# Layer norms 1 to 3: the low part of the turned tokens by a TensorE product with a negative unit matrix and a ScalarE copy, in place of a VectorE subtraction

## What is computed

```python
x = L0_attn_data                                   # 1024 x 512, fp32
x = x + _L0_attn_ref(_layernorm(x), ...)           # product with a block-masked weight, 512 x 512
x = x + _L0_ffn_ref(_layernorm(x), ...)            # product with an int4 weight, and a bias
x = x + _L1_attn_ref(_layernorm(x), ...)           # NF4 weights with low-rank terms: (q+k+v)/3, out, gate/up, down
x = x + _L1_ffn_ref(_layernorm(x), ...)            # FP4-rounded activations and weights, gated MLP
```

## Time and profile before

| what | us |
|---|---|
| time, median of 3 runs | 836.36 (834.82 to 837.74) |
| the profiled execution, its own time | 842.19 |
| its span (first to last instruction) | 840.8 |
| PE busy | 722.5 (86%) |
| DVE busy | 582.3 (69%) |
| ACT busy | 430.1 (51%) |
| POOL busy | 191.4 (23%) |
| mean granted TensorE clock | 0.945 of full speed |

### The profile page before, as it was taken

The page is one execution under the profiler, slowest core; times in us unless marked ns, Lnnn a source line. Parts: engine busy times, 40 slices in busy tenths (PEclk is TensorE's granted clock), DMA queues, the critical chain, the costliest instruction groups (busy, mean ns, idle before and its releaser), DMA issues.

```text
span 840.8 us, 11246 instructions
## 1 busy us (share of the span) xinstructions
PE 722.5 (86%) x4112; PEld 537.4 (64%) x4112; DVE 582.3 (69%) x1107; ACT 430.1 (51%) x549; POOL 191.4 (23%) x176
## 2 busy tenths in 40 slices
PE   1796755878999998989998999778999799959998
PEld 1564421656777766667665777566777588957886
DVE  4899978644598788889897984568363333567873
ACT  3765747457777767877656511264322221225452
POOL 0213000003253452635544543222001200000000
PEclk9999966799999999999998999989899899988999
DMA  8644668767366686758755110211001210200001
GB/s 279 214 140 154 204 209 268 264 218 244 111 193 208 198 246 208 237 175 265 222 166 161 62 47 27 62 39 53 23 1 38 60 47 26 76 10 12 26 26 38
DMA packets 56040, 110.55 MB, mean 131 GB/s; under 512 B 9889, under 2 KB 20801, under 8 KB 55985
## 3 DMA queue, kind: packets, MB, share of 16 engines
q1 hardware_dynamic: 42560, 78.43, 28.9%
q10 hardware_dynamic: 9040, 17.30, 6.1%
q0 software_dynamic: 4384, 14.09, 5.9%
HBM read 91.65 MB, written 18.15 MB: 131 GB/s over the span
## 4 chain that ended last, share of the span: by engine, by line
PE 51%; DVE 27%; issue 8%; DMA 6%; ACT 6%; SPq 1%; ACTq 0%; DVEq 0%
PE bank L1106 13%; PE bank L1107 13%; PE bank L1108 13%; DVE hot L1747 3%; PE bank L1213 2%; DMA wide_buf<-in_down_flat 2%; DVE bank L1773 2%; ACT hot L1501 2%; DVE x L1870 2%; PE bank L1394 2%; PE bank L1226 1%; DVE q_a L1820 1%; DMA codes<-c 1%; DVE q_r L1814 1%; DVE gm L1789 1%
## 5 line engine op out<-in xcount | busy, mean ns | idle before, releaser
L1501 ACT ACTIVATE hot<-rep,levels 128x2048 f16<-128x2048 f16 x96 | 193.6, 2056 | 19.7 <-ACT c L1464 10.1
L1106 PE MATMUL bank<-zt_h,w_h 128*128 128x512 f32 (+1 forms) x232 | 93.2, 402 | 2.5 <-DVE zt_l L1858 2.0
L1108 PE MATMUL bank<-zt_h,w_l 128*128 128x512 f32 (+1 forms) x232 | 91.2, 393 | 0.0
L1107 PE MATMUL bank<-zt_l,w_h 128*128 128x512 f32 (+1 forms) x232 | 91.0, 392 | 0.0
L1213 PE MATMUL bank<-hot,diag 128*32 128x512 f16 x1160 | 79.2, 399 | 8.2 <-DVE hot L1747 5.6
L1106 PE MATMUL bank<-w_h,xq_h 128*128 128x512 f32 (+1 forms) x192 | 75.4, 393 | 5.8 <-DVE w_l L1888 3.5
L1107 PE MATMUL bank<-w_l,xq_h 128*128 128x512 f32 (+1 forms) x192 | 73.5, 383 | 0.0
L1108 PE MATMUL bank<-w_h,xq_l 128*128 128x512 f32 (+1 forms) x192 | 73.1, 381 | 0.0
L2013 POOL TENSOR_TENSOR q_a<-q_a,q_m 128x384 f32<-128x384 f32 (+3 forms) x34 | 35.7, 1050 | 109.2 <-DVE q_m L1641 109.2
L1213 PEld LDWEIGHTS bank<-hot,diag 128*32 128x32 f16 x1160 | 26.1, 98 | 52.2 <-issue 26.0
L1106 PE MATMUL bank<-w_h,at_h 128*128 128x512 f32 x112 | 48.3, 431 | 7.8 <-DVE x L1870 5.0
(11 more groups left out here) (219 smaller groups left out, 1674.8 us busy)
## 6 DMA issues: line engine op xcount, KB each, us to landing
rep<-codes SPq DMA_DIRECT2D x58, 512.0 KB, 4.6
codes<-c SPq DMA_DIRECT2D x29, 256.0 KB
raw<-in_codes_gu_t ACTq DMA_DIRECT2D x14, 512.0 KB, 4.6
sc<-in_scales_gu_t SPq DMA_DIRECT2D x56, 128.0 KB, 4.4
raw<-in_codes_attn_t ACTq DMA_DIRECT2D x8, 512.0 KB, 4.7
raw<-in_codes_down_t ACTq DMA_DIRECT2D x7, 512.0 KB, 5.7
sc<-in_scales_down_t SPq DMA_DIRECT2D x28, 128.0 KB, 3.0
wide_buf<-in_gate_flat SPq DMA_DIRECT2D x5, 512.0 KB, 4.7
```

Source lines behind the costliest of these rows:

```text
L1106: PE.matmul(psum, lh, rh, start=first, stop=False, **kw)
L1107: PE.matmul(psum, lh, rl, start=False, stop=False, **kw)
L1108: return PE.matmul(psum, ll, rh, start=False, stop=last, **kw)
L1501: S.activation(hots[plan.slot[hot_ring(t), (t, m)]][:], codes_in_place(t), ACT.Relu, bias=bias, scale=slope).then_inc(sem("ramp_act"), 1)
```

## The change

For layer norms 1 to 3 (`ln < PE_LOWS`, which is 3) the DVE subtraction is gone. A new step `tlow` has two halves. On PE one matmul with the matrix `minus` (minus one on the diagonal) and `zt_h` of this tile adds `-zt_h` to the bank that holds the turned tile; the four transposes of the tile are now an open group of accumulation for this. On ACT a copy then takes the bank, which now holds the low part, into `zt_l`. The bank comes free after that ACT copy, and `product` and `o_mm` wait for it. In the list of steps `tsplit` of tile n-1 now stands ahead of `norm` of tile n+1, and `tlow` behind it. Layer norm 4 keeps the DVE subtraction, under the name `tdiff`. `minus` is built at the start of the program, and no longer at the start of the last phase.

```diff
+PE_LOWS = 3
+def split_done(ln, n):
+    return ("act", "tlow", ln, n) if ln < PE_LOWS else ("dve", "tdiff", ln, n)
...
             p.add("turn", ln, n)
-            turn_bank(("ln", ln, n), ("dve", "tsplit", ln, n))
+            turn_bank(("ln", ln, n), split_done(ln, n))
+            if ln < PE_LOWS and turned is not None:
+                p.add("tsplit", ln, turned)
             if n + 1 < NT:
                 norm(ln, n + 1)
+            if ln >= PE_LOWS and turned is not None:
+                p.add("tsplit", ln, turned)
             if turned is not None:
-                p.add("tsplit", ln, turned)
+                p.add("tlow" if ln < PE_LOWS else "tdiff", ln, turned)
                 yield turned
             turned = n
...
                 for k in range(KD):
                     cols = slice(256 * (k // 2) + k % 2, 256 * (k // 2) + 256, 2) if ln == 1 else tok(k)
-                    last = PE.transpose(bank[:, tok(k)], z[:, cols], ident)
+                    last = PE.matmul(bank[:, tok(k)], z[:, cols], ident, start=k == 0 or ln >= PE_LOWS,
+                                     stop=ln >= PE_LOWS, is_transpose=True, skip_group_check=True)
                 last.then_inc(sem("turn_pe"), 1)
+            elif kind == "tlow":
+                ln, n = key
+                pe.wait_ge(*done("dve", "minus"))
+                pe.wait_ge(*done("act", "tsplit", ln, n))
+                PE.matmul(turned_view(turn(("ln", ln, n)), P, 0, KD), minus[:], zt_h[:, :, tok(n)], start=False,
+                          stop=True, skip_group_check=True).then_inc(sem("tlow_pe"), 1)
             elif kind == "product":
-                pe.wait_ge(*done("dve", "tsplit", blk_no - 1, n))
+                pe.wait_ge(*done(*split_done(blk_no - 1, n)))
...
+            elif kind == "tlow":
+                ln, n = key
+                act.wait_ge(*done("pe", "tlow", ln, n))
+                S.copy(zt_l[:, :, tok(n)], turned_view(turn(("ln", ln, n)), P, 0, KD)).then_inc(sem("tlow_act"), 1)
...
-            elif kind == "tsplit":
+            elif kind == "tdiff":
                 ln, n = key
                 dve.wait_ge(*done("act", "tsplit", ln, n))
```

More of the change, by code:

```diff
@@ L563, in make_plan @@
     p.sends("const_in", "const", 3)
+    p.add("minus")
     p.add("mask_load")
@@ L690, in make_plan @@
     p.turn_in4 = set()
-    p.add("minus")
     def norm4_rest():
@@ L920, in build @@
     ident = ident_r[:].bitcast(F32)
+    minus = sb("minus", [P, P], F32R)
     levels, diag = sb("levels", [P, 5], F32), sb("diag", [P, 256], F16)
@@ L964, in build @@
         w_last = sb("w4_h", [P, 1, 512], F32R, late), sb("w4_l", [P, 1, 512], F32R, late)
-        minus = sb("minus", [P, P], F32R, late)
     wraw = wide_buf[:].rearrange("p (k n) -> p k n", k=KD)
@@ L1292, in pe_program @@
                 bank, cols = o_bank(half, o), half_of(half)
-                pe.wait_ge(*done("dve", "tsplit", 2, HN * half + HN - 1))
+                pe.wait_ge(*done(*split_done(2, HN * half + HN - 1)))
                 for m in vacant("main", ("o", *key)) if o != 3 * (1 - half) else turn_vacant(("o", *key)):
@@ L1346, in pe_program @@
                 bank = main4(("p", n))
-                pe.wait_ge(*done("dve", "tsplit", 3, n))
+                pe.wait_ge(*done("dve", "tdiff", 3, n))
                 pe.wait_ge(*done("dve", "perm"))
@@ L1368, in pe_program @@
                 pe.wait_ge(*done("pool", "lr"))
-                pe.wait_ge(*done("dve", "tsplit", 3, NT - 1))
+                pe.wait_ge(*done("dve", "tdiff", 3, NT - 1))
                 for m in vacant("main4", ("la", half)):
@@ L1705, in dve_program @@
                 V.tensor_tensor(zt_l[:, :, tok(n)], turned_view(turn(("ln", ln, n)), P, 0, KD), zt_h[:, :, tok(n)],
-                                ALU.subtract).then_inc(sem("tsplit_dve"), 1)
+                                ALU.subtract).then_inc(sem("tdiff_dve"), 1)
             elif kind == "add":
@@ L1880, in dve_program @@
             elif kind == "minus":
+                dve.wait_ge(*done("dve", "const"))
                 V.tensor_scalar(minus[:], ident, -1.0, None, ALU.mult).then_inc(sem("minus_dve"), 1)
```

## The result

| what | before | after |
|---|---|---|
| time, median of 20 runs each | 842.32 us (834.82 to 849.34) | 836.16 us (830.93 to 841.37) |
| ratio after to before, 95% interval | | 0.994 (0.9915 to 0.9965) |
| the profiled execution, its own time | 842.19 | 835.99 |
| its span | 840.8 | 834.7 |
| mean granted TensorE clock | 0.945 | 0.951 |

By the ratio the change makes the kernel faster by 0.6%, some 5 us, with 3 to 7 inside the interval. The two medians differ by 6.2 us, and so do the two profiled executions. The prediction's difference of 7 us is at the edge of that interval. Its absolute time of 829.4 is 7 us too low: it was taken from a median of three runs, 836.36, and 20 runs of the same kernel have a median of 842.32.

What follows compares the result with a forecast made beforehand. The prediction took VectorE to set the pace of the edited stage, with TensorE close behind in its first third. Gains of 2 + 4 + 1 = 7 us from a median of 836.36 gave 829.4 us, range 823 to 838.

Steps and rivals of the forecast that it cites:

- the three stretches: Edited stage: gains of 2 us to 65 us, 4 from 65 to 112, and 1 from 112 to 137.
- What it removes: VectorE, from 36.8 us: 21 subtractions, 12.6 us, plus 7.0 us of idle time; 19.6 us as upper bound.
- Edits at nothing: Small edits, such as early `minus`, open transposes and cast ahead of norm, were given no gain beyond idle times counted.
- To 65 us: Block 1: VectorE sheds 4.2 us, TensorE ends 3.6 late; last add near 63.6, gain 2 us, bounds minus 3.6 to 4.2.
- 65 to 112 and 112 to 137 us: Later stretches: gains of 4 us (bounds 0 and 6.15) and 1 us (0 and 1.8), as ScalarE fills up.
- the sign that the prediction itself set: Stage end some 7 us earlier: last copy into `zt_l` near 130 us, where the last subtraction was at 136.09.
- The second is wrong: Test of the 65 to 112 us term, forecast at 4 us: it fails if the gain does not grow there.
- The new waits: TensorE waits for ScalarE's cast 2 to 6 us in all, ScalarE's copy for the `minus` matmul 5 to 10.
- Rival C: Slower: TensorE's `minus` matmul waits over 1.4 us at each of 14 ramps; at 1.75 us, 841.3 us; chance 0.12.
- Rival B: Hand-over eats the gain: copy and hop show at each of 21 tiles, 0.5 us left, 835.9 us; chance 0.18.
- The rule on the port: VectorE and POOL share a port lock: two hot planes more or fewer under POOL's adds, 0.85 us each.
- Carrying over: From 137 us to the end: the gain at 137 us is the gain at the end, within 2 us.

Runs made afterwards that it cites:

- e1: Kernel before with only the order changed: ScalarE's cast ahead of the next tile's norm in layer norms 1 to 3, VectorE's subtraction kept; 0.9921 of before.
- e11: Changed kernel with the old order, the next tile's norm ahead of the cast; matmul with `minus` and copy kept; 1.0001 of before.
- e17: Changed kernel with ScalarE's square root of layer norms 1 to 3 right behind its statistics; 0.987 of before.
- e8: Kernel before with the four transposes of each tile made twice in layer norms 2 and 3; 1.0011 of before.
- e5: Changed kernel with each tile's cast in the step in which it was turned, ahead of that step's ramp; 0.9915 of before.
- e10: Changed kernel without any low part in layer norms 1 to 3, its array staying zero; 0.9832 of before.
- e13: Changed kernel with VectorE's subtraction back in layer norm 1; matmul and copy only in norms 2 and 3, new order in all three; 0.9864 of before.
- e19: Changed kernel with the edits of e17 and e5 together; 0.9866 of before.
- e3: Changed kernel with layer norm 1 put back as before; matmul, copy and new order in norms 2 and 3 only; 0.9878 of before.
- e4: Changed kernel with ScalarE's square root right behind its statistics in all four layer norms; 0.9908 of before.
- e14: e13 with ScalarE's square root of layer norms 1 to 3 right behind its statistics; 0.9894 of before.

## Why the prediction was right and where it was wrong

**The size and the sign.** 7 us were predicted; 6.2 lie between the profiled pair and 5 by the ratio. The terms behind it were 2, 4 and 1 us for the three stretches. In the traces the gain is 0.1 us at block 1's last add, 5.5 at block 2's (105.49 to 100.03) and 6.1 at the merge. The sum came near by luck: the first term was 2 too high, the other two together 1 too low, and the gain came mostly by a cause to which the prediction had given no price. The forecast of 829.4 us had a second fault: its starting value, 836.36, lies 6.0 us under the median of 20 runs.

**What was removed.** The step that failed is under "What it removes": it counts 21 x 0.60 us of work and 7.0 us of idle time as leaving VectorE "with the instruction", 19.6 us as one quantity. They are two. The idle time left VectorE in e1, where every subtraction is still there: 7.0 us became 3.6, and 5.0 us came off the merge. The 12.6 us of work left in e11 and gave nothing. "Edits at nothing" had the sentence with the answer in it, that the cast ahead of the norm lets a cast go when the norm has to wait for `known`, and gave it nothing beyond the idle times counted. The price could be read in the trace of before: three waits of 1.35 us on VectorE (32.05, 70.45, 112.67), each behind a cast that stood behind such a norm, and the second in the very term for 65 to 112 us. The two parts of a diff should have been summed apart, each as if the other weren't there.

The premise under it was too wide as well. The prediction had the chain of waits run along VectorE, instruction after instruction, and from 40 to 69 us it does, but for one square root. But behind the cast that was held until 69.86 it goes over to TensorE for 10 us, in `lora`, transposes, product and `look`; the first and the last piece are

```profile
73.94 0.47 PE bank L1226
...
83.45 0.79 PE bank L1213 x12
```

VectorE is the next link at 84.29, and from 117 us on the chain runs along TensorE and ScalarE for most of the way. During these 10 us before 84.29 work taken from VectorE shortens no link, and at their start TensorE is at its lower clock: matmuls of 512 columns start 0.43 us apart (75 to 78 us), and 0.23 apart behind that. So the 0.40 us that the prediction took as the upper bound of one such matmul was too low too.

**To 65 us.** TensorE came as forecast: the look behind block 1's last product starts at

```profile
62.33 1.26 PE L1225 MATMUL bank<-hot,diag 128*32 128x512 f16 x20
```

where 62.4 was predicted and 58.82 stood before. But the last add did not follow from it at 63.6:

```profile
62.38 1.65 DVE L1770 TENSOR_SCALAR hot<-rep,levels 128x2048 f16<-128x2048 f16 x1
63.95 1.65 DVE L1773 TENSOR_SCALAR hot<-rep,levels 128x2048 f16<-128x2048 f16 x1
65.53 0.67 DVE L1734 TENSOR_TENSOR x<-x,bank 128x512 f32<-128x512 f32 x1
```

The two hot planes stand 0.5 us later than they stood, since VectorE had shed six subtractions by then, 3.6 us, and lost 3.61 us at the square root and 1.66 us in a wait for TensorE at block 1's third add. The wait at the square root isn't in the prediction, which followed what is queued behind TensorE's new wait, but not what is queued on ScalarE behind the new copy. e17 shows the price, 6.1 us at the merge.

**65 to 112 and 112 to 137 us.** 4 and 1 us were predicted, 5.4 and 0.6 came if the merge is taken as the end of the stage. By the sign that the prediction itself set it came short: the last copy into `zt_l` starts at 133.72, near 130 was forecast, and the last subtraction stood at 136.09. From 36.8 to 137 us VectorE's busy time fell by 9.3 us, where 14 were forecast, since later work moved in; ScalarE's rose by 13.3 (11 to 13). In the third stretch VectorE waits 6.7 us in all for the high parts of the weights on ScalarE, a wait that the trace of before has not, which fits the prediction's reading that ScalarE can't follow there. "The second is wrong if the gain does not grow from 65 to 112 us": it grew. That ScalarE limits the stretch fits e11's chain; that TensorE has room, 15 and 10 us by the prediction, fits e8.

**The new waits.** TensorE's for the cast was forecast at 2 to 6 us and is 13.8; e5 shows that this costs about 1 us at most, so the price of 0.4 us per ramp was too low as a wait and not too low as a cost. ScalarE's for the matmul was forecast at 5 to 10 and is 12.2. Rival C, "slower" from 1.4 us for each ramp, named a true wait: 13.8 us over the 14 ramps that it counted is 1.0 us each; but its sum took a wait of TensorE as time of the kernel, which e5 refutes. Rival B (the hand-over eats it) is what happens to the move alone, in e11, though by ScalarE's list and not by a copy and a hop at each tile.

**The rule on the port.** The last two planes before 65.53 took 1.65 us each again, at POOL's adds, so at this place the shifted times brought neither of the two prices that the prediction set beside it. Further on, two planes less fell under POOL's adds: those at 73.70 and 80.45 took 1.20 and 1.34 us before, and in the changed kernel none from 70 to 86 us took over 0.81. That is 1.0 us less on VectorE, but at a time at which the chain ran along TensorE. On the other rule, that work may go to ScalarE when VectorE is saturated (the Trainium skill, Perfetto Trace Analysis, Optimizing Scalar/DVE Operations): VectorE was saturated by its busy time, and e11 shows that the move by itself gave nothing, because the chain then ran through ScalarE's ramp, norm and cast.

**Carrying over.** The gain is 6.1 us at the merge, 5.7 at the last down add and 6.2 at the end, so this step holds. For larger gains it holds less well: 12.2, 9.9 and 10.4 in e17, 15.8, 13.5 and 14.1 in e10. About 2 us stay behind between the merge and 540 us; what takes them was not looked into.

## What to carry to other kernels

When a change both moves work to another engine and reorders a queue, cost the two apart; here the reordering alone gave what the whole change gave, by letting one cast go that stood behind a norm with a wait of its own. An instruction moved onto an engine's queue delays all behind it, and a tiny one there (a square root of 0.2 us) can hold another engine for 3.6 us. The order is right only for a given load: the early square root gave 6.1 us with the move in layer norm 1 and cost 1 to 2 without it. And 14 us of waits on an engine that is not the limit were worth about 1 us, no more than the spread.

Three versions beat both kernels: e13, e17 and e19 at 0.9864 to 0.987 of before, against 0.994. They can't be told apart by their times, and e3's 0.9878 (0.9823 to 0.9933) can't be told from theirs.

## What the runs showed of the hardware

The stretch from the last down add to the last add takes 289.0 to 289.6 us in 15 of the 18 traces. It takes 292.5 in e4, 285.1 in e13 and 285.3 in e14. All of this lies ahead of the add at 629.1 us in before (L1908): from there to the last add it is 208.9 to 209.3 us in all 18. e4's excess comes from norm 4's square root, as shown above. What sets e13 and e14 apart is the granted clock (the third number from the right). Here are the same 24 us, from 36 to 60 us behind the last down add, in e3 and in e13:

```profile
577.30:601.30 24.00, 21.49 (x78) 16.36 (x79) 10.02 (x18) 8.66 (x17) 3.33 (x4) 0.79 0.15 44
```

```profile
575.80:599.80 24.00, 21.53 (x96) 16.40 (x97) 13.74 (x26) 9.50 (x19) 3.17 (x3) 1.00 0.16 44
```

TensorE is busy as long in both, but with 78 matmuls in one and 96 in the other. In both kernels it had just stood idle twice in the same way, for 1.64 and 0.68 us in e3 and for 1.65 and 0.68 in e13; behind that the clock fell to its lower level in e3 and stayed at full speed in e13 and e14. That gives e13 and e14 back 4 us, nearly as much as the change, and e13's lead over e3 at the end (824.9 to 830.5, where their merges are 0.2 us apart) is mostly this. Why these executions kept the clock, and whether their programs bring it about by when they reach the stretch, stays open.
